# Causal masks added by VectorE instead of TensorE, with a rewritten order of the head loop, and the closing layer norms cut into pieces

## What is computed

```python
# part 1, for each of 2 x 16 heads
sim = where(causal_mask, -max, (q * scale) @ k.T)      # 1024 x 1024, above the diagonal masked
attn = softmax(sim)
out = attn @ v
adj = clip(attn + eye, 0, 1); deg = sum(adj)
feats = v
for l in range(2):
    feats = gelu(adj @ (feats @ gnn_w[l] + gnn_b[l]) / deg + feats)
out = out + feats @ lin_w + lin_b
x1 = layer_norm(concat(out) @ Wo)
# part 2, for each of 2 layers
x = x + local_attention(rotary(l2norm(q)), rotary(l2norm(k)), v) @ wo
h = layer_norm(shift_token(x)) @ w1 + b1
x = x + (a * gelu(g)) @ w2 + b2                        # a, g: halves of h, 341 wide
# after each part: a layer norm and the sum with the input
```

## Time and profile before

| | us |
|---|---|
| median of 3 runs | 1490.47 (1489.58 to 1495.8) |
| profiled execution | 1495.98 |
| its span, first to last instruction | 1494.2 |
| TensorE matmul busy | 1379.5 (92%) |
| VectorE busy | 1193.5 (80%) |
| ScalarE busy | 996.4 (67%) |
| GpSimd busy | 363.8 (24%) |

### The profile page before, as it was taken

How to read it: one execution, slowest core, us unless ns; L and a number is a source line. 1 busy time by engine, 2 the same in 40 slices (tenths; PEclk the granted TensorE clock), 3 DMA queues, 4 the chain that set the end, 5 groups by cost and what they waited for, 6 DMA issues and landing times. The chain is left out here.

```text
span 1494.2 us, 28152 instructions
## 1 busy us (share of the span) xinstructions
PE 1379.5 (92%) x9560; PEld 1067.2 (71%) x9560; DVE 1193.5 (80%) x3498; ACT 996.4 (67%) x2376; POOL 363.8 (24%) x442
## 2 busy tenths in 40 slices
PE   5899999999999999999999999998878999999895
PEld 3577887788778878778778778776556666666663
DVE  5388888888887888888888888775888888888875
ACT  3367776677667767767667766774566787778573
POOL 1023122221222112212232123212322332222211
PEclk9699999999999999999999999998799999999999
DMA  5012111211111111211112111310310010101100
GB/s 137 1 33 54 38 30 29 45 42 30 29 44 43 30 29 35 52 30 29 29 44 44 30 30 43 84 34 12 92 23 13 21 23 19 22 19 23 29 12 21
DMA packets 40664, 53.25 MB, mean 36 GB/s; under 512 B 11678, under 2 KB 23882, under 8 KB 40522
## 3 DMA queue, kind: packets, MB, share of 16 engines
q1 hardware_dynamic: 40522, 51.46, 15.0%
HBM read 9.89 MB, written 1.05 MB: 7 GB/s over the span
## 5 line engine op out<-in xcount | busy, mean ns | idle before, releaser
L1151 ACT ACTIVATE t<-PS 128x512 f32<-128x512 f32 (+3 forms) x384 | 190.5, 496 | 172.2 <-PE PS L689 116.2
L1651 DVE TENSOR_TENSOR t<-t 128x512 fp32r<-128x512 f32 (+3 forms) x384 | 210.0, 554 | 7.8 <-ACT t L1152 7.1
L1152 ACT ACTIVATE t<-PS 128x512 fp32r<-128x512 f32 (+3 forms) x384 | 190.5, 496 | 0.0
L739 PE MATMUL PS<-t 128*128 128x512 f32 (+3 forms) x384 | 144.6, 377 | 22.4 <-ACT t L1185 22.1
L1308 ACT ACTIVATE t<-PS,t 128x128 f32<-128x128 f32 x256 | 113.3, 464 | 68.0 <-DVE t L1903 68.0
L686 PE MATMUL PS<-t 128*128 128x512 f32 (+3 forms) x384 | 145.4, 379 | 4.8 <-DMA t<-t 2.2
L1484 POOL TENSOR_TENSOR t<-t 128x16 f32<-128x16 f32 x32 | 92.8, 2902 | 234.1 <-DVE t L1752 234.1
L660 PE MATMUL PS<-t 128*128 128x512 f32 (+3 forms) x384 | 141.0, 383 | 6.5 <-DVE t L1634 3.6
L1448 POOL TENSOR_TENSOR t<-t 128x256 f32<-128x256 f32 x64 | 39.4, 615 | 401.3 <-DVE t L1671 401.3
L704 PE MATMUL PS<-t 128*66 128x512 f32 (+3 forms) x384 | 135.2, 352 | 0.0
L687 PE MATMUL PS<-t 65*128 65x512 f32 (+3 forms) x384 | 134.6, 350 | 0.0
(11 more groups left out here) (206 smaller groups left out, 3687.7 us busy)
## 6 DMA issues: line engine op xcount, KB each, us to landing
t<-t SPq DMA_DIRECT2D x184, 128.0 KB, 2.3
t<-t SPq DMA_DIRECT2D x62, 256.0 KB, 3.4
t<-in_c_rot SPq DMA_DIRECT2D x4, 512.0 KB, 5.5
t<-in_L_ffn_wqkv SPq DMA_DIRECT2D x2, 768.0 KB, 6.0
t<-in_L_attn_Wv SPq DMA_DIRECT2D x2, 512.0 KB, 7.6
out<-t SPq DMA_DIRECT2D x4, 256.0 KB, 2.3
t<-in_L_ffn_w SPq DMA_DIRECT2D x2, 341.0 KB
t<-in_L_attn_x SPq DMA_DIRECT2D x2, 256.0 KB, 3.3
```

The lines of the kernel that those rows point to most:

```text
L739: e.matmul(dst, F2[:, jb, :], Eh[:, o:o + n], start=(jb == 0), stop=False)
L1151: e.activation(Es[:, k % NS, 0:n], b[:, 0:n], ACT.Exp).then_inc(a_es.up((t, k)), 1)
L1152: e.activation(Eh[:, o:o + n], b[:, 0:n], ACT.Exp).then_inc(a_eh.up((t, k)), 1)
L1651: e.tensor_tensor(El[:, o:o + n], Es[:, k % NS, 0:n], f32(Eh[:, o:o + n]), ALU.subtract).then_inc(d_el.up((t, k)), 1)
```

## The change

- **Masks.** The matmul L689 and its constant `cmB` go. VectorE has a new step `acausal(t, k)` (L1659 of the new kernel), which adds the float32 mask to the first 128 columns of a diagonal tile in PSUM, in place. ScalarE's Exp of such a tile waits for it (`d_sm`) and no more for TensorE. VectorE does it eight times per head.
- **Order of the head loop.** The steps of TensorE, ScalarE and VectorE within an iteration are put in another order; apart from the masks none is added or dropped. On VectorE `share(t-1, 1)`, `tail` and the steps `scores` stand later and `smax` mostly earlier; on TensorE `graph2(t-1, 10)` and `graph1(t, 0)` stand later; on ScalarE `share`, `hopend`, `av` and `mrow` stand later.
- **Layer norms within the block loop.** `finish` becomes `finish_stats` and `finish_rest`. For group 4 they stand at k = 26 and k = 27 and for group 5 at k = 30 and k = 31, so the power on GpSimd falls between them.
- **The last group.** In `down(7)` the first two blocks of rows go to bank 7 and the last two to bank 0, each with its own semaphore, and VectorE adds, norms and stores them as two halves (groups "7" and "7.5"). `gate` and `up` of group 7 alternate on TensorE; the product goes to other memory (`pt`), and ScalarE takes Gelu straight from PSUM (`gated`), with no pass through Identity.

```diff
@@ tensor: scores, and the head loop
                 b = bank(2 + k % 2)
-                diag = jb >= 4 * c
                 e.matmul(b[:, 0:n], K1[r][:, jb * P:(jb + 1) * P], Q1[r][:, i0:i0 + n], start=True, stop=False)
-                m = e.matmul(b[:, 0:n], K2[r][:, jb * P:(jb + 1) * P], Q2[r][:, i0:i0 + n], start=False, stop=not diag)
-                if diag:
-                    m = e.matmul(b[:, 0:P], identB[:], cmB[:, 1, :], start=False, stop=True)
-                m.then_inc(p_sc.up((t, k)), 1)
+                e.matmul(b[:, 0:n], K2[r][:, jb * P:(jb + 1) * P], Q2[r][:, i0:i0 + n], start=False,
+                         stop=True).then_inc(p_sc.up((t, k)), 1)
...
-                graph2(t - 1, 10)
-                scores(t, 3)
                 tailT(t - 2, 0)
...
@@ tensor: down, and the end
+                        dst = bank(b if g < NG - 1 or r < 2 else 0)
+                        m = e.matmul(dst[:, r * P:(r + 1) * P], pt(g, c)[0:n, r * P:(r + 1) * P], w2[l][0:n, c, :],
                                      start=(c == 0), stop=(c == 2))
-                m.then_inc(p_dn.up(g), 1)
+                    if g == NG - 1 and r == 1:
+                        m.then_inc(p_dn.up(g), 1)
+                m.then_inc(p_dn.up(g if g < NG - 1 else g + 0.5), 1)
...
             gate(7, 0, 0, d_rm[NA - 1])
+            up(7, 0, 4, d_up[6, 1])
             gate(7, 1, 1, d_rm[NA - 1])
+            up(7, 1, 5, d_up[6, 2])
             gate(7, 2, 2, a_gate[6, 2])
+            up(7, 2, 6, a_sh[7])
             down(6, 3, d_up[6, 0])
-            up(7, 0, 4, d_up[6, 1])
-            up(7, 1, 5, d_up[6, 2])
-            up(7, 2, 6, a_sh[7])
             down(7)
@@ scalar: scores
-                q.wait_ge(*p_sc[t, k])
                 q.wait_ge(*(d_el[t, k - NS] if k >= NS else d_el[t - 1, k + NTL - NS]))
                 q.wait_ge(*p_hop[t - 1, k])
+                q.wait_ge(*(d_sm if jb >= 4 * c else p_sc)[t, k])
@@ vector: the new step
+            def acausal(t, k):
+                if t >= NH:
+                    return
+                q.wait_ge(ld["cm"], 16)
+                q.wait_ge(*p_sc[t, k])
+                s = bank(2 + k % 2)[:, 0:P]
+                e.tensor_tensor(s, s, cm[:, 1, :], ALU.add).then_inc(d_sm.up((t, k)), 1)
@@ vector: the block loop and the end
-                if k == 26:
-                    finish(4)
...
                 add(k - 1)
+                if k in (26, 30):
+                    finish_stats(k // 4 - 2)
+                if k in (27, 31):
+                    finish_rest(k // 4 - 2)
             norm(7)
+            q.wait_ge(*d_rot[NA - 1])
+            q.wait_ge(*d_ss[NA - 1])
+            e.memset(pt(7, 2)[64:P, :], 1.0).then_inc(d_fz.up("PT7"), 1)
             for c in range(3):
                 up(6, c, 3 + c)
-            finish(5)
-            down(6, 3)
             for c in range(3):
                 up(7, c, 4 + c)
-            finish(6)
+            down(6, 3)
+            finish_stats(6)
             down(7)
-            finish(7)
+            finish_stats(7)
+            finish_rest(6)
+            down(7.5, 0)
+            finish_stats(7.5)
+            finish_rest(7)
+            finish_rest(7.5)
```

More of the change, by code:

```diff
@@ L542, in sync @@
             finish(7)
-            e.wait_ge(s_out, 16 * 4)
+            finish(7.5)
+            e.wait_ge(s_out, 16 * 5)
         def tensor(e):
@@ L838, in tensor @@
                     linear(0, 7)
-                scores(t, 4)
-                smax(t + 1, 0)
-                smax(t + 1, 1)
+                scores(t, 3)
                 tailT(t - 2, 1)
-                av(t, 0)
                 smax(t + 1, 2)
@@ L846, in tensor @@
                     linear(1, 6)
-                tail(t - 2, 0)
+                av(t, 0)
+                scores(t, 4)
                 smax(t + 1, 3)
@@ L851, in tensor @@
                 scores(t, 5)
-                scores(t, 6)
+                tail(t - 2, 0)
                 smax(t + 1, 4)
@@ L855, in tensor @@
                     linear(3, 6)
+                scores(t, 6)
                 tail(t - 2, 1)
@@ L1262, in scalar @@
                     linear(4, 6)
+                projv(t + 1, 1)
+                hopend(t - 1, 1)
+                proj(t + 2, 0, 2)
                 scores(t, 11)
@@ L1269, in scalar @@
                 share(t, 0)
-                mrow(t + 1)
                 gelu2(t - 1)
@@ L1273, in scalar @@
                     square(0)
+                mrow(t + 1)
                 hopend(t, 0)
@@ L1831, in vector @@
                     linear(0, 7)
+                acausal(t, 3)
+                scores(t, 1)
+                scores(t, 2)
+                smax(t + 1, 2)
                 scores(t, 3)
-                smax(t + 1, 2)
+                smax(t + 1, 3)
+                scores(t, 4)
+                smax(t + 1, 4)
                 tail(t - 2, 0)
-                smax(t + 1, 3)
-                smax(t + 1, 4)
                 tail(t - 2, 1)
-                scores(t, 4)
                 smax(t + 1, 5)
-                scores(t, 5)
-                scores(t, 6)
-                smax(t + 1, 6)
-                projv(t + 1, 0)
                 if 2 <= t < 6:
@@ L1848, in vector @@
                     onward_stats(2 * ((t - 18) % 4), (t - 18) // 4, 2)
-                scores(t, 7)
-                scores(t, 8)
-                scores(t, 9)
-                if t == 0:
-                    linear(5, 7)
+                acausal(t, 8)
+                scores(t, 5)
+                smax(t + 1, 6)
                 if 2 <= t < 6:
@@ L1857, in vector @@
                     onward_rest(2 * ((t - 18) % 4), (t - 18) // 4, 2)
+                share(t - 1, 1)
+                scores(t, 6)
+                projv(t + 1, 0)
+                scores(t, 7)
+                acausal(t, 9)
+                acausal(t, 10)
+                smax(t + 1, 7)
+                scores(t, 8)
+                smax(t + 1, 8)
+                scores(t, 9)
+                if t == 0:
+                    linear(5, 7)
                 projv(t + 1, 1)
                 scores(t, 10)
-                smax(t + 1, 7)
+                acausal(t, 11)
+                smax(t + 1, 9)
                 graph1(t, 0)
                 scores(t, 11)
-                smax(t + 1, 8)
+                lower(t + 2, 0, 2)
+                feats(t, 0)
                 graph2b(t - 1)
-                feats(t, 0)
-                smax(t + 1, 9)
-                lower(t + 2, 0, 2)
+                smax(t + 1, 11)
                 lower(t + 2, 1, 3)
-                smax(t + 1, 11)
                 smax(t + 1, 10)
```

133 lines of the change are left out of this document (74 added, 59 removed).

## The result

| | before | changed |
|---|---|---|
| median us (runs) | 1490.03 (4, 1489.38 to 1495.8) | 1476.06 (4, 1475.51 to 1477.01) |
| profiled execution | 1495.98 | 1476.47 |
| its span | 1494.2 | 1474.7 |

The ratio is 0.9898, 95% interval 0.9873 to 0.9924: 1.0% faster. The forecast was 1472.8 within 1457 to 1488, and faster with 0.70.

A forecast was written before the change was run, and what follows sets the result against it. TensorE was taken to bound iterations without `projv`, VectorE close behind. Head loop -15.6, block loop -0.8 and end -1.3 sum to -17.7 us, taking the median from 1490.47 to 1472.8 us, range 1457 to 1488.

The forecast's parts named there:

- The mask on TensorE, 0.12 us: Head loop: each mask costs TensorE 0.04 us itself and 0.08 for the type change behind it; eight give 1.0 us.
- rival 2: Head loop: only 0.04 us per mask is saved on TensorE, the 0.08 turns up elsewhere; 1485 us, chance 0.12.
- The mask on VectorE, a slot of 0.20: Head loop: each mask takes VectorE 0.20 us; two of eight are free, six add 1.2 us per iteration.
- TensorE's floors of 30.9 and 27.4: Head loop: TensorE's least us per odd and even iteration without masks, down from about 31.9 and 28.4.
- one allowance of 0.45 us per iteration for all: Head loop: time above the larger engine floor because the engines find each other late, 14.4 us over 32 iterations.
- Rival 1: Head loop: VectorE bounds iterations with layer norm pieces, a pair 61.5 us, other pairs gain 1.2; 1481 us, chance 0.18.
- Block loop, -0.8: Block loop: splitting `finish(4)` and moving `finish(5)` into the loop together save 0.8 us.
- `finish(4)` -1.3: Block loop: in two pieces, its 1.12 us wait for GpSimd and the hand-over go, some -1.3 us.
- `finish(5)` +0.5: Block loop: its 1.5 us of statistics stand before block 31's first step, which had 0.97 us idle, so +0.5.
- The end, -1.3: End of the program: the last sum ends at 1490.1 instead of 1491.44 us, -1.3 us.
- Rival 3: Head loop: TensorE waits for Exp, Exp for a mask in VectorE's queue; 0.6 us per iteration, 1508 us, chance 0.10.
- the second sign: Head loop, a sign that the forecast is wrong: TensorE waits of more than 1 us per iteration.

The follow-up runs named there:

- e2: Changed kernel with the masks given back to TensorE, new order kept: 1486.26 us, 0.9968 of the kernel before.
- e4: Changed kernel with the mask of the scores left out altogether (computes another function): 1472.87 us, 0.9878 of the kernel before.
- e11: Changed kernel with VectorE's `share` put ahead of the layer norm pieces and the masks of the scores left out: 1462.46 us, 0.9793 of the kernel before.
- e5: Changed kernel with the layer norms of groups 4 and 5 whole again, group 5 behind up(6): 1473.95 us, 0.9865 of the kernel before.
- e6: Changed kernel with the layer norm of group 5 one block later: 1475.93 us, 0.9881 of the kernel before.
- e1: Kernel before with only the masks moved from TensorE to VectorE, old order of steps: 1578.85 us, ratio 1.061.
- e10: Kernel before with the masks on VectorE, old order of other steps, each mask as early as its tile allows: 1647.08 us, ratio 1.1035.

## Why the prediction was right, and where it was not

**The mask on TensorE, 0.12 us: right in size, with a condition that I had not stated.** Between e2 and e4 eight masks are worth 0.69 us (iteration 14) and 1.22 (13), 0.09 to 0.15 each; with pieces, where other things hold the iteration, only 0.51 (20) and 0.47 (21). The rule of the Trainium skill (VectorE: DVE Perf Modes, section on the TRN2 errata), estimated 0.056 us, gives 0.45 us for eight; without pieces the measurement decides against it. In the old order the same masks gave 0.51 (iteration 14) and 0.12 (13), near rival 2's figure, but in the even iteration that was read by another mechanism: its 0.08 does not turn up at another change of type, TensorE waits for banks.

**The mask on VectorE, a slot of 0.20: right.** The rows show 0.20. The Trainium skill (Perfetto Trace Analysis, Optimizing Scalar/DVE Operations) led to an estimated 0.26, which the row does not bear out; the recorded duration of 0.298 overlaps the successor. That its 1.2 us would raise VectorE's floor without setting the iteration held where no pieces are (0.09 and 0.22 us in 14 and 13).

**TensorE's floors of 30.9 and 27.4.** Measured: 30.41 and 27.48. The even one is met to 0.1. The odd one was undercut, since the 31.9 it started from held something that the order removes (e2: 0.53 less with the masks still on TensorE). I had also read that TensorE waits "at one place" in eight iterations; the view has a second, L725 for VectorE's `projv` step L1617, 0.7 us in each odd iteration with pieces. That is most of the 0.85 by which iteration 19 lay above 13, and in the changed kernel TensorE still waits 0.8 for that step.

**The step that failed: one allowance of 0.45 us per iteration for all.** Without pieces none of it was needed: a pair takes 57.9 where its floors are 58.3, and gains 2.4 us, not 1.2. With pieces it was too little: iterations 20 and 21 take 60.9, 1.4 above my floors of 59.5, nearly all of it in the even one (29.24 against 28.1, the odd one 31.66 against 31.4), and 18 to 29 together lose 0.8 us where I had -4.8. Rival 1 described these iterations better (its pair of 61.5 against 60.9, and e11 shows the masks on VectorE holding the even ones), but not the rest, which gained twice its 1.2. The loop's total, -14.64 against -15.6, came right because the two errors are of opposite sign, and that is luck.

**What the forecast missed.** First, a wait can cost more than its length: in iterations 18 and 24 a wait of 1.5 us came with 1.4 us more each at the lower clock, and block 30 took 1.5 us more than the term for `finish(5)`. Second, the two ends of the head loop, which I put at nothing, moved by -4.83 and +1.95.

**The sum.** In the profiled executions the parts that I had priced came to -14.64, +0.13 and -2.1, together -16.6 where I had -17.7; with the two ends it is -19.5. I took the sum off the median, and the medians differ by 14.0, because the profiled execution before lay 5.95 us above its median and the changed one 0.4 above. So the median missed the forecast by 3.3 us, though the profiles differ by more than I forecast. These errors have both signs, and that the time came so close is in part luck; the direction, the price of a mask on either engine and the need for the new order are not.

**Block loop, -0.8: +0.13.** `finish(4)` -1.3: measured -1.4 (e5 against e6). `finish(5)` +0.5: the softmax of block 31 starts 0.35 later, near the forecast, but the sum of block 30 comes 2.0 later, at the lowered clock; how much of the 2.0 is the clock and how much the longer wait (2.64 for 2.32), no run separates.

**The end, -1.3.** Measured -1.6, from the sum of block 31 to the end of the last sum. That `finish(5)` "had been free there" holds: e5, which has it behind the loop again, takes as long from the sum of block 31 to the end of its span (26.3 us) as the changed kernel. Which of the other edits of the end gives the 1.6, no run takes apart.

**Rival 3 (slower: the mask in the round of the score banks)** is no accident of an unlucky kernel but what this change is without its order: +88 and +155 us in e1 and e10, not +19. That VectorE's "queue seldom comes to an input that is not there" was the argument for the order, and e10's waits show what happens where it does. Its chance of 0.10 rested on the new order being good, for which I had only the gap sizes.

**What was to be seen.** Iterations of 27.8 and 31.3 without pieces: 27.48 and 30.41. 28.6 and 31.8 with: 29.2 and 31.66. VectorE's gaps were to close; windows of whole iterations, 13, 14 and 20 (third group: VectorE):

```profile
425.61:456.02 30.41, 29.73 (x194) 25.21 (x193) 27.00 (x91) 22.65 (x53) 7.58 (x12) 1.00 0.16 35
456.02:483.50 27.48, 26.80 (x171) 22.63 (x171) 24.51 (x86) 20.26 (x45) 6.14 (x10) 1.00 0.18 40
...
636.08:665.32 29.24, 27.12 (x171) 22.63 (x171) 26.25 (x94) 20.41 (x44) 6.86 (x11) 1.00 0.17 37
```

Idle on VectorE, the turn included, are 3.4, 3.0 and 3.0 us, where the same iterations of the kernel before left 5.9, 5.1 and 4.5: VectorE is busier by the masks and idles less. Of the three signs against, none came without pieces; with them TensorE waits 1.4 to 1.5 us for `share` in iterations 18, 20, 22 and 24, the second sign, and there the forecast was indeed wrong.

## What to carry to other kernels

In this kernel, work moved from a full engine to one nearly full cost little only where its input was there when the queue came to it and its reader did not wait yet; the same eight instructions were worth +88, +155 or -10 us by their place and that of their neighbours. So cost such a move together with its order, and keep separate allowances for stages in which the receiving engine is full and for those where it is not. And a wait of 1.5 us on TensorE is to be priced with what the clock does behind it.
